# adaLN block on one Trainium2 core: first normalisation on ScalarE from tile 4 on, and tile 6 turned ahead of the column sums

## What is computed

```python
def reference(...):
    mod = (_silu(L0_c) @ L0_wmod).reshape(L0_c.shape[0], 6, 1, -1)
    sa, ca, ga, sb, cb, gb = (mod[:, k] for k in range(6))
    h = _layernorm(x, axis=-1) * (1 + ca) + sa
    x = x + ga * attn(h)      # h @ w.T + bias; w is masked in 32 x 32 blocks, 1024 x 1024
    h = _layernorm(x, axis=-1) * (1 + cb) + sb
    x = x + gb * ffn(h)       # down(silu(gate(h)) * up(h)), integer weights with scales, 2752 wide
    return x
```

## Time and profile before

| | |
|---|---|
| time before, median of 3 runs | 1158.65 us (1157.67 to 1162.24) |
| the profiled execution's own time | 1155.59 us |
| its span in the profile | 1153.8 us |
| mean granted TensorE clock | 0.985 of full speed |
| busy share of the span | PE 95%, PEld 44%, DVE 67%, ACT 37%, POOL 41% |

### The profile page before, as it was taken

The page is one execution under the profiler, slowest core; times in us unless marked ns, Lnnn a source line. Parts: engine busy times, 40 slices in busy tenths (PEclk is TensorE's granted clock), DMA queues, the critical chain, the costliest instruction groups (busy, mean ns, idle before and its releaser), DMA issues. The chain is left out here.

```text
span 1153.8 us, 13073 instructions
## 1 busy us (share of the span) xinstructions
PE 1096.0 (95%) x4629; PEld 513.3 (44%) x4629; DVE 770.0 (67%) x966; ACT 427.1 (37%) x776; POOL 476.2 (41%) x453
## 2 busy tenths in 40 slices
PE   5997999999998888999899999999999999999998
PEld 3553454545443333444344434444444444444444
DVE  4889957766677776878778868678655433344434
ACT  0321146656464444435455545555443000000000
POOL 1223337447645463545586857677442000000000
PEclk9998989999999999999999999999999999999999
DMA  9993221435333547445566565665359866655440
GB/s 348 403 360 74 74 62 49 109 96 169 137 147 121 143 119 204 134 119 153 160 181 188 160 202 170 192 186 174 105 203 375 339 239 230 239 230 202 181 160 37
DMA packets 94288, 206.93 MB, mean 179 GB/s; under 512 B 18576, under 2 KB 54160, under 8 KB 91792
## 3 DMA queue, kind: packets, MB, share of 16 engines
q1 hardware_dynamic: 78176, 145.81, 38.5%
q0 software_dynamic: 16048, 60.30, 15.5%
HBM read 137.39 MB, written 68.68 MB: 179 GB/s over the span
## 5 line engine op out<-in xcount | busy, mean ns | idle before, releaser
L1291 PE MATMUL pA<-work 128*128 128x512 f16 x1680 | 383.6, 383 | 25.3 <-ACT work L1032 17.8
L1291 PEld LDWEIGHTS pA<-work 128*128 128x128 f16 x1680 | 163.4, 99 | 233.2 <-ACT work L1032 27.3
L1154 PE MATMUL pA<-work 128*128 128x512 f32 x512 | 227.0, 598 | 0.7 <-issue 0.7
L1291 PE MATMUL pB<-work 128*128 128x512 f16 x752 | 177.3, 381 | 4.3 <-DVE work L1722 4.3
L1744 DVE SCALAR_TENSOR_TENSOR work<-work 128x512 f16<-128x512 f16 x144 | 133.8, 930 | 50.5 <-ACT work L1050 50.1
L1154 PEld LDWEIGHTS pA<-work 128*128 128x128 f32 x512 | 96.4, 193 | 113.2 <-issue 112.3
L1358 PE MATMUL pA<-work 128*128 128x512 f16 x600 | 134.4, 379 | 0.0
L907 ACT ACTIVATE work<-pB,small 128x128 f32<-128x128 f32 x256 | 92.6, 480 | 90.3 <-PE pB L1143 77.0
L1291 PEld LDWEIGHTS pB<-work 128*128 128x128 f16 x752 | 73.7, 98 | 94.4 <-DVE work L1722 5.8
L829 POOL DMA_DIRECT2D h_scratch<-work x80 | 62.1, 790 | 124.9 <-DVE work L1744 124.7
L1050 ACT ACTIVATE work<-work 128x512 f16<-128x512 f32 x144 | 88.1, 625 | 67.8 <-DMA h_scratch<-work 26.3
(11 more groups left out here) (173 smaller groups left out, 1190.3 us busy)
## 6 DMA issues: line engine op xcount, KB each, us to landing
work<-h_scratch SPq DMA_DIRECT2D x8, 4480.0 KB, 13.8
h_scratch<-work POOLq DMA_DIRECT2D x60, 512.0 KB, 4.0
work<-in_L_wmod SPq DMA_DIRECT2D x10, 2048.0 KB, 18.1
work<-in_L_ffn_gate_w SPq DMA_DIRECT2D x84, 128.0 KB, 4.8
work<-in_L_ffn_up_w SPq DMA_DIRECT2D x84, 128.0 KB, 2.9
work<-down_scratch SPq DMA_DIRECT2D x7, 1280.0 KB, 17.0
work<-in_L_ffn_down_w SPq DMA_DIRECT2D x68, 128.0 KB, 3.3
work<-in_L_attn_data SPq DMA_DIRECT2D x16, 512.0 KB, 4.3
```

The lines of the kernel that those rows point to most:

```text
L1154: last = pe.matmul(pA[:, 2 * par(t) + h, :], hT1[par(t)][:, c, :], wT[:, c, h * H:(h + 1) * H], start=(c == 0), stop=(c == KT - 1))
L1291: last = pe.matmul(ps, w[:, m, c], bc[b][:, mv_, s, c], start=begin, stop=(i == n - 1 and c == KT // 2 - 1 and s == 1), skip_group_check=True)
```

## The change

From tile 4 on (`BY_ACT = 4`) the first normalisation is an activation on ACT, `z1 = rstd * x + shift`, in the new function `normalise_first`. It stands in ACT's list in iteration `t` for tile `t + 2`, right behind `turn_out(t + 1)` and ahead of the second inputs and high parts. Its `shift = -(mean * rstd)` is made on POOL behind each `rstd` by two more operations on 128 x 1. DVE's `normalise(0, t)` falls away for these 12 tiles. `mv`, `rstd` and `shift` of the first statistics get six places, and POOL and DVE get waits that guard their reuse. In PE's list `transpose(0, 6)` now stands ahead of the two `columns` of iteration 5.

```diff
@@ -476,8 +480,11 @@
+        BY_ACT = 4
...
@@ -724,10 +731,18 @@
             def rstd_of(L, n):
+                if L == 0 and n >= BY_ACT + 2:
+
+                    pool.wait_ge(z_done[0], n - 1)
                 pool.wait_ge(mv_done[L], n + 1)
                 pool.tensor_tensor(ve[L], mv[L][place(n)][:, 1:2], eps, ALU.add).then_inc(ve_done[L], 1)
                 pool.wait_ge(ve_done[L], n + 1)
                 pool.tensor_tensor(rstd[L][place(n)], ve[L], mhalf, ALU.pow).then_inc(rstd_done[L], 1)
+                if L == 0 and n >= BY_ACT:
+                    pool.wait_ge(rstd_done[L], n + 1)
+                    pool.tensor_tensor(shift_step, mv[L][place(n)][:, 0:1], rstd[L][place(n)], ALU.mult).then_inc(shift_done, 1)
+                    pool.wait_ge(shift_done, 2 * (n - BY_ACT) + 1)
+                    pool.tensor_tensor(shift[place(n)], shift_step, minus, ALU.mult).then_inc(shift_done, 1)
...
@@ -911,6 +926,11 @@
+            def normalise_first(t):
+                act.wait_ge(shift_done, 2 * (t - BY_ACT + 1))
+                act.wait_ge(t_done[0], t)
+                act.activation(z1, xt[par(t)], ACT.Identity, scale=rstd[0][place(t)], bias=shift[place(t)]).then_inc(z_done[0], 1)
...
@@ -1002,6 +1022,8 @@
                 if t <= LAST - 1:
                     turn_out(t + 1)
+                if BY_ACT <= t + 2 <= LAST:
+                    normalise_first(t + 2)
                 if t == 13:
                     hi_part(t - 3)
...
@@ -1255,13 +1277,13 @@
                     attend(t, 0)
+                if t <= LAST - 1:
+                    transpose(0, t + 1)
                 if t == 5:
 
                     pe.wait_ge(pair_free, 3)
                     for v in (3, 4):
                         columns(v, colp2[:, KT * (v - 3):KT * (v - 2)])
-                if t <= LAST - 1:
-                    transpose(0, t + 1)
...
@@ -1458,6 +1480,8 @@
             def normalise(L, t):
+                if L == 0 and t >= BY_ACT:
+                    return
...
@@ -1470,6 +1494,8 @@
             def stats1(t):
                 dve.wait_ge(x_loaded[par(t)], 16 * (t // 2) + 16)
+                if t >= BY_ACT + 2:
+                    dve.wait_ge(shift_done, 2 * (t - 1 - BY_ACT))
                 stats(0, t, xt[par(t)])
```

More of the change, by code:

```diff
@@ L33, in adaln_kernel @@
     W_MAX = 128.0
-    SMALL = 232
+    SMALL = 240
     LAST = NT - 1
@@ L239, in adaln_kernel @@
         bnst = [cols(12) for _ in range(2)]
-        mv = [[cols(2)] * 6, [cols(2) for _ in range(6)]]
+        mv = [[cols(2) for _ in range(6)], [cols(2) for _ in range(6)]]
         ve = [cols(1) for _ in range(2)]
-        rstd = [[cols(1)] * 6, [cols(1) for _ in range(6)]]
+        rstd = [[cols(1) for _ in range(6)], [cols(1) for _ in range(6)]]
         mhalf = cols(1)
@@ L246, in adaln_kernel @@
         two = cols(1)
+        minus = cols(1)
+        shift = [cols(1) for _ in range(6)]
+        shift_step = cols(1)
         share = cols(1)
@@ L319, in adaln_kernel @@
         rstd_done = [sem(f"rstd_done{k}") for k in range(2)]
+        shift_done = sem("shift_done")
         z_done = [sem(f"z_done{k}") for k in range(2)]
@@ L478, in adaln_kernel @@
         SUMS_AT = {6: 1, 7: 3, 8: 5, 10: 7, **{t: t - 2 for t in range(11, LAST + 1, 2)}}
-        NCONST = 13
+        NCONST = 14
         block = ctx.enter_context(nc.Block())
+        BY_ACT = 4
         def par(t):
@@ L713, in _ @@
             pool.wait_ge(consts_set, 8)
-            for v, value in ((mhalf, -0.5), (eps, EPS), (one, 1.0), (two, 2.0), (share, 1.0 / P)):
+            for v, value in ((mhalf, -0.5), (eps, EPS), (one, 1.0), (two, 2.0), (minus, -1.0), (share, 1.0 / P)):
                 pool.memset(v, value).then_inc(consts_set, 1)
```

## The result

The change takes 1162.60 us (median of 12 runs, 1156.56 to 1165.37); the kernel before, on the same chips, 1157.13 us (12 runs). The ratio is 1.004, 95% interval 1.0021 to 1.006: **4.6 us slower** (2.4 to 6.9). (The times here are the ratio's distance from 1 times the median of before; the two medians themselves lie 5.5 us apart.) A second series, beside the experiments, gave 1.0037 (1.0016 to 1.0058), 4.3 us. So it is slower, but by less than the 0.5% within which the forecast would have called it no change, and it had given 0.68 to more than that. The forecast of 1168.0, 9.3 us over before, had the sign and twice the size.

A forecast was written before the change was run, and what follows sets the result against it. PE, busy 95% of the span, was taken as the bound. Gains of 4.1 and 0.5 us were netted into +7.8 at tile 7's turn; with +0.5 and +1.0 that made +9.3 on 1158.65: 1168.0 us, range 1158.5 to 1176.

The forecast's parts named there:

- the ring: Second input, POOL's sums, high part, low part, statistics, deviation and shift, ACT's normalisation, next second input: each waits for the last.
- The first rival: Second inputs are ready in time, so PE keeps its gains: 6.3 us faster, 1152.4 us; chance 0.12.
- the second rival: Less contention between POOL and DVE shortens three rounds by 9.6 us: -0.3, 1158.3 us; chance 0.20, including results up to +5.8.
- the signs: PE gaps of 4 to 5 us before tile 4's turn (iteration 7), 7 to 10 before tile 7's (iteration 9).
- Slower still: Longer shift products, clock, iteration 13, unshrunk sums and smaller lead add 6.6 us: 1174.6 us, the forecast's upper end.
- Tile 4: PE's first gap, before tile 4's turn, ends at 108.1 instead of 112.2: -4.1 us (-4.3 to -3.5).
- Tile 6's turn: Turned ahead of the column sums, it takes half of 1.95 us: -0.5 us (bounds -0.9 and +0.5).
- PE's lead: From iteration 6 on PE would be 4.6 us ahead of the kernel before.
- The rounds: Three rounds after second_input(1), sums to deviation 16.45, 15.85 and 15.58 us, each plus 1.8 for shift and normalisation.
- The turn of tile 7: At iteration 9's end it starts at 237.85 instead of 225.41, 12.4 us late, less 4.6: +7.8 us.
- Clock and iteration 13: Half clock behind the gap before tile 7's turn, +1.0 (0 to 2.3); tile 15's deviation holding ACT's list, +0.5 (0 to 1.6).

The follow-up runs named there:

- act_late: The change with ACT's normalisation of tiles 8 to 15 moved behind the second inputs in ACT's list; ratio 0.9936 to the kernel before, 7.4 us faster.
- early_only: The change with only tiles 4 to 7 normalised on ACT, tiles 8 to 15 on DVE again; ratio 0.9935 to the kernel before, 7.5 us faster.
- dose4: The change with four more one-column products on POOL ahead of each shift from tile 8 on; ratio 1.0114 to the kernel before, 13.2 us slower.
- mixed_pool4: The change with normalisations of iterations 6 to 9 behind second inputs, and POOL making tile 4's deviation and shift before tile 3's bias sum; ratio 0.9909 to before.
- to9: The change with only tiles 4 to 8 normalised on ACT; ratio 0.9964 to the kernel before, 4.2 us faster.

## Why the prediction missed, step by step

**The mechanism held.** A ring closed through ACT's list; PE stood before the turns of tiles 4 and 7, released by the second input; the sums start 20.8 and 20.0 us after one another. act_late shows the cause by moving the waiting instruction alone, early_only by having no ring, dose4 by its multiple. The first rival (the ring stays open) is out: with it the stage is 7 us shorter, not 5.7 longer. The result fell into the band that I had given the second rival, but not by its mechanism: the rounds shrank by 1.7 us in all, not by 9.6. Of the signs that I had named, the gap before the turn of tile 4 came as said (4.29 us), but the one before tile 7's was 5.06 us and not 7 to 10: the 3.9 us that it lacks of the expected 9 are the larger lead (2.2) and the shorter rounds (1.7), both below. One slip in the recorded sum changes nothing: the terms of "Slower still" add up to 6.4, not 6.6.

**Tile 4: -4.1 predicted, -3.5 measured**, at the end of its range. POOL's shift took until 110.18 from the power's end at 108.97, 1.2 us for the pair where I took 0.7, since both ran beside DVE. POOL's timeline with the change:

```profile
108.21 0.76 POOL L740 TENSOR_TENSOR small<-small 128x1 f32<-128x1 f32 x1
109.06 0.33 POOL L743 TENSOR_TENSOR small<-small 128x1 f32<-128x1 f32 x1
109.47 0.71 POOL L745 TENSOR_TENSOR small<-small 128x1 f32<-128x1 f32 x1
```

The activation took 1.24, not 1.1. The half-speed stretch stayed, as said.

**Tile 6's turn: -0.5 predicted, -3.3 measured. This is the step that failed.** I wrote of the products that "directly behind the column sums they may all run at half", so that the order would change only the turn's own time. That the turn itself takes half ahead of the column sums was right (1.04 us). But in both profiles of the change everything behind it ran at full clock too. The kernel before had this in the same stretch, against 1.00 in the change:

```profile
148.00:152.00 4.00, 4.00 (x14) 3.00 (x14) 2.48 (x9) 1.43 (x5) 0.37 (x2) 0.50 0.72 206
```

PE's lead at iteration 6, the time by which it is ahead of before, was 3.5 + 3.3 = 6.8 us, not 4.6. My bounds (-0.9 to +0.5) took the half-speed stretch as given and moved work about inside it; that it could be there in one execution and absent in the next was not among them.

**The rounds: 21.2, 20.6 and 20.3 predicted, 20.84, 19.94 and 19.67 measured**, 1.7 us too long together. From the start of the sums to the deviation they are 16.16, 15.27 and 14.98 us where I had 16.45, 15.85 and 15.58. I carried over the low part's duration in each round of before, 2.68 us in the first and 2.25 and 2.20 in the others. With the change it takes 1.60 each time (L1556 on DVE's timeline; L1507 is the residual of the same round):

```profile
172.83 1.69 DVE L1507 TENSOR_TENSOR work<-work 128x1024 f32<-128x1024 f32 x1
...
181.26 1.60 DVE L1556 TENSOR_TENSOR work<-work 128x1024 f16<-128x1024 f32 x1 [3.71 <-ACT work L985]
```

POOL's bias sum now begins at 179.41 and is nearly over when the low part starts; before, it began at 181.56 and lay beside it. So the low parts give 2.3 us in the three rounds, and the sums 0.5 beyond what I had taken off. POOL's deviation takes 1.4 of that back, 0.5 in each round: before, DVE's next first normalisation waited for POOL's power and left it undisturbed (0.56 us); with the change DVE goes straight on to its second normalisation, and in the first two rounds the power beside it takes 1.02. From DVE's timeline, beside the power at 187.30:

```profile
187.09 0.81 DVE L1493 TENSOR_SCALAR work<-work,small 128x1024 f32<-128x1024 f32 x1
```

So contention did give a little back, mainly because the bias sum and the low part slid apart. By the timelines, the normalisation that left DVE also gave the power a neighbour that it hadn't had. Where they still meet the price is the old one: POOL's L774 took 2.13 us beside DVE's residual L1507, against 1.26 at 194.35, where DVE stood idle for most of it. The Trainium skill (GPSIMD Engine Reference, section 1, Specifications) names VectorE instructions with two SBUF inputs as one of two kinds that contend with GpSimd. L1507 is one, and with the normalisation gone from DVE the trace agrees with that rule.

**The turn of tile 7: +7.8 predicted, +4.5 measured** (126.22 us after the first gap's start instead of 121.71). The miss of 3.3 is the lead, 2.2, and the rounds, 1.7, less some 0.5 by which the ring started and ended later than the sum had it.

**Clock and iteration 13: +1.0 and +0.5 predicted, +1.2 together measured** (the stage behind the turn of tile 7 is 95.29 us instead of 94.09). Iteration 13 made no wait. The clock's half-speed stretch behind the last gap was 3.4 us long. That the clock loss of the gap before (8.72 us for the products at 194.80 instead of 7.03, and 0.87 in the turn) vanishes in the ring was right.

The terms as measured, -3.5 - 3.3 + 11.3 + 1.2, make the 5.7 us of the stage, where 11.3 is the turn of tile 7 without PE's lead. Against the forecast's 9.3 that is 3.6 less: 2.8 from tile 6's turn, 1.1 from the ring and 0.3 behind it, less 0.6 that tile 4 fell short (rounded terms). The timed runs say 4.6 and 4.3, and 5.7 lies within their intervals.

## What to carry to other kernels

When work moves to an idle engine, ask what stands behind it in that engine's list and what it waits for: an instruction that waits for a result which itself needs the work queued behind it closes a ring, and the ring's length, not the engine's busy share, is then the time. Put the waiting instruction behind everything that is ready earlier, or move only those tiles whose result PE really waits for; here either turned +4.6 us into about -7.5. And where a stretch at half clock stands behind short work, its presence is an uncertainty of some 3 us in both directions, which belongs into the range of every edit that touches it.

## What was unexpected of the hardware

- **The clock behind the 16 matmuls of one column is no fixed property of the program.** PE is busy throughout (4.00 of 4.00 us in each stretch), and yet in 6 of 12 profiles the granted clock went to 1.2 GHz there for 6.8 us (3.4 in mixed_pool4, where PE had a gap of 0.29 us ahead of them). The same instructions took 17.93 us to the next turns in the change and 21.28 in dose4.
- **What a gap costs in clock doesn't follow its length.** After the gap of 5.04 at tile 4 PE worked at half speed for 4.8 us (from 111.5 to 116.3), after the 8.50 of before for 4.6 (from 112.2 to 116.8), after the 3.25 of mixed_pool4 for 3.1 (from 110.5 to 113.6). Over the nine profiles with a gap of 5.0 there it was 4.3 to 5.1 us. But in the change it was 3.05 us behind the gap of 5.06 before the turn of tile 7, and 5.1 behind the shorter gap of 4.29. Behind the gaps of 1.6 to 1.9 us there was no such stretch in any profile, behind the 2.58 of to9 one of 3.4.
- **Beside some of DVE's work POOL's operations on one column take several times as long.** In the change the shift product L745 took 0.19 us as a rule and 0.71 beside the row sums (L1584); the power L740 took 0.55, 1.02 beside DVE's normalisation and 1.43 beside its low parts (L1558 and L1560). DVE being busy is not enough: at 104.48 the power took 0.56 beside the statistics, and at 228.28 L745 took 0.19 beside L1519, which reads PSUM.
